# Attention: the diagonal blocks of the second pass masked by a bf16 product ahead of the exponential

## The reference, cut to what matters

```
att = einsum('bhqd,bhkd->bhqk', q, k) / scale
att = where(tril, att, -inf);  att = softmax(att, axis=-1)
y = einsum('bhqt,bhtd->bhqd', att, v)
x = x + (y @ Wo.T + bo)
```

## Time and profile before

| | us |
|---|---|
| median of 3 runs | 3162.8 |
| lowest and highest of them | 3155.71, 3166.08 |
| the profiled execution, its own time | 3170.36 |
| its span, first to last instruction | 3168.4 |
| the second pass of attention in it | 156 to 316.7 |
| TensorE busy | 2841.4 (90%) |
| VectorE, ScalarE, GpSimd busy | 1743.9, 1548.3, 361.7 |

### The profile page before, as it was taken

One profiled execution on the slowest core, in us unless ns is written; L12 is line 12 of the kernel. 1 busy time (PEld: TensorE's weight loads), 2 busy tenths in 40 slices (PEclk: granted clock), 3 DMA queues, 4 the chain that ended last, 5 costly groups with the idle time before them and its releaser, 6 DMA issues. The chain is left out here.

```text
span 3168.4 us, 79399 instructions
## 1 busy us (share of the span) xinstructions
PE 2841.4 (90%) x31700; PEld 2180.3 (69%) x31700; DVE 1743.9 (55%) x4255; ACT 1548.3 (49%) x3945; POOL 361.7 (11%) x731
## 2 busy tenths in 40 slices
PE   7899879999659999999999999989999998689998
PEld 4433559999526777677676677767767767579997
DVE  4443556666245556556555555655655555476663
ACT  1123222322136676677667667667666766422221
POOL 0011000000002111111111111111111111000000
PEclk9889889999779999999999999999999999889999
DMA  1000012010000000000000000000000000011100
GB/s 44 25 1 1 26 42 81 27 53 26 5 28 5 12 12 16 5 12 16 5 16 12 16 5 12 15 5 12 15 6 15 12 6 6 26 57 53 50 30 13
DMA packets 58891, 65.34 MB, mean 21 GB/s; under 512 B 16064, under 2 KB 50256, under 8 KB 58576
## 3 DMA queue, kind: packets, MB, share of 16 engines
q1 hardware_dynamic: 58576, 60.92, 6.2%
HBM read 59.86 MB, written 1.05 MB: 19 GB/s over the span
## 5 line engine op out<-in xcount | busy, mean ns | idle before, releaser
L1362 PE MATMUL dn_ps<-xnT,dn_w 128*128 128x512 f32 x768 | 378.9, 619 | 18.7 <-issue 11.5
L433 ACT ACTIVATE g_h<-g_ps,g_b_now 128x512 f32<-128x512 f32 x256 | 174.9, 688 | 338.3 <-PE g_ps L457 332.5
L1446 PE MATMUL dn_ps<-dn_zi,dn_wt 64*64 64x64 f32 x5120 | 262.3, 226 | 50.2 <-DVE dn_zi L1800 50.0
L470 PE MATMUL g_ps<-g_w_high,g_h_low 128*128 128x256 f32 x1024 | 290.3, 283 | 0.0
L470 PE MATMUL g_ps<-g_w_low,g_h_high 128*128 128x256 f32 x1024 | 290.2, 283 | 0.0
L470 PE MATMUL g_ps<-g_w_high,g_h_high 128*128 128x256 f32 x1024 | 290.1, 283 | 0.0
L1446 PEld LDWEIGHTS dn_ps<-dn_zi,dn_wt 64*64 64x64 f32 x5120 | 210.7, 139 | 77.1 <-DVE dn_zi L1800 51.9
L1800 DVE TENSOR_TENSOR dn_zi<-dn_ps,dn_mz 128x128 f32<-128x128 f32 x640 | 159.7, 286 | 186.3 <-PE dn_ps L1436 182.1
L1533 ACT ACTIVATE dn_qs<-dn_ps,dn_cf 64x128 f32<-64x128 f32 x448 | 162.3, 362 | 203.3 <-DVE dn_wv L1810 198.8
L1741 DVE SCALAR_TENSOR_TENSOR dn_cv<-dn_raw,dn_cw,dn_cv 128x1024 f32<-128x1024 f32 x192 | 247.5, 1289 | 2.0
L1810 DVE SCALAR_TENSOR_TENSOR dn_wv<-dn_ps,dn_cf,dn_vt 64x128 f32<-64x128 f32 x448 | 156.6, 349 | 147.8 <-PE dn_ps L1461 142.9
(11 more groups left out here) (267 smaller groups left out, 5980.2 us busy)
## 6 DMA issues: line engine op xcount, KB each, us to landing
g_w<-in_fc_dram SPq DMA_DIRECT2D x32, 1024.0 KB, 6.6
dn_w<-in_W_qkvz_dram SPq DMA_DIRECT2D x16, 768.0 KB, 4.4
dn_wout<-in_W_out_dram SPq DMA_DIRECT2D x16, 256.0 KB, 2.6
f_gate<-in_gateT_dram SPq DMA_DIRECT2D x16, 128.0 KB, 2.2
f_up<-in_upT_dram SPq DMA_DIRECT2D x16, 128.0 KB, 2.4
f_down<-in_downT_dram SPq DMA_DIRECT2D x16, 128.0 KB, 2.4
x_res<-in_x_dram SPq DMA_DIRECT2D x1, 1024.0 KB, 5.0
out_dram<-x_res SPq DMA_DIRECT2D x1, 1024.0 KB, 4.7
```

The costliest lines, as they stand in the source:

```text
L433: nc.scalar.activation(h[:, f % 4], h_b[f % 4], ACT.Gelu, bias=b1_now[u // 2][:, f:f + 1]).then_inc(h_ready, 1)
L470: last = pe.matmul(y_b[q % 2][:, 0:D], hidden[:, f, q * P:(q + 1) * P], weights[:, f, :], start=(f == 0 and n == 0), stop=(f == NF - 1 and ...
L1362: mm = pe.matmul(bA if where == "A" else bC, w[:, k, W_COL[u] * P:(W_COL[u] + 1) * P], m.xnT[:, k, b * T:(b + 1) * T], start=(k == 0), sto ...
L1446: mm = pe.matmul(block_of(bD[s], 1, b, h), wt[s][half(h), 1, b, :], zi[s][half(h), b, :], start=True, stop=True)
```

## The change

The table of constants gets an eighth block, the transposed causal mask. It is loaded and cast beside the first. The key side's scores leave their PSUM group open and two bf16 products, identity by transposed mask, are added onto the diagonal block ahead of the exponential; they give `sT_ready`. The masks of both sides become steps of their own, which stand behind both score products. GpSimd's loop of selections and its semaphore are gone; the value products wait for `e_ready`.

```diff
-    table = np.concatenate([eye, causal, tri, ones, last, last0, last1], axis=1)
+    table = np.concatenate([eye, causal, tri, ones, last, last0, last1, causal.T], axis=1)
...
+        maskT = sb("maskT", [P, P], BF16)
...
-            LOADS = 8 + 2 * HKV
+            LOADS = 9 + 2 * HKV
...
                 sp.dma_start(mask_in[:], const(table, C_CAUSAL)).then_inc(loaded, 16)
+                sp.dma_start(maskT_in[:], const(table, C_CAUSAL_T)).then_inc(loaded, 16)
...
                 nc.gpsimd.tensor_copy(mask[:], mask_in[:]).then_inc(padded, 1)
+                nc.gpsimd.tensor_copy(maskT[:], maskT_in[:]).then_inc(padded, 1)
...
+
+                def mask_rows(n):
+                    t = n % HT
                     for i in range(2):
                         mm = pe.matmul(slot(rows_place(n))[:, i, t * P:(t + 1) * P], ident[:], mask[:], start=False, stop=True)
                     mm.then_inc(s_ready, 1)
...
-                        mm = pe.matmul(slot(keys_place(n))[:, i, 0:T - j * P], kT[rows, b * T + j * P:b * T + (j + 1) * P],
-                                       qT[rows, r, b * T + j * P:(b + 1) * T], start=True, stop=True)
+                        pe.matmul(slot(keys_place(n))[:, i, 0:T - j * P], kT[rows, b * T + j * P:b * T + (j + 1) * P],
+                                  qT[rows, r, b * T + j * P:(b + 1) * T], start=True, stop=False)
+
+                def mask_keys(n):
+                    for i in range(2):
+                        mm = pe.matmul(slot(keys_place(n))[:, i, 0:P], ident[:], maskT[:], start=False, stop=True)
                     mm.then_inc(sT_ready, 1)
 
                 def values(n):
                     pair, b, r, gp, j = item(n)
-                    pe.wait_ge(p_ready, n + 1)
+                    pe.wait_ge(e_ready, n + 1)
...
                 for n in range(AHEAD):
                     rows_of_scores(n)
+                    mask_rows(n)
...
                         keys_of_scores(n)
                     if n + AHEAD < ITEMS:
                         rows_of_scores(n + AHEAD)
+                    if n < ITEMS:
+                        mask_keys(n)
+                    if n + AHEAD < ITEMS:
+                        mask_rows(n + AHEAD)
...
-                for n in range(ITEMS):
-                    pool.wait_ge(e_ready, n + 1)
-                    diagonal = pT[n % PT_BUFS][:, :, 0:P]
-                    nc.gpsimd.affine_select(diagonal, diagonal, [[0, 2], [1, P]], ALU.is_ge, 0.0, base=0,
-                                            channel_multiplier=-1).then_inc(p_ready, 1)
```

## The result

The changed kernel took 3179.78 us (median of 7 runs, 3173.06 to 3181.26) against 3166.08 (7 runs, 3155.71 to 3173.92): a ratio of 1.0042, 95% interval 1.0025 to 1.0059. A second set, with the changed kernel run again, gave 3176.17 against 3165.89, ratio 1.0032, interval 1.0017 to 1.0047. So the change costs 0.3 to 0.4% (the two intervals together reach from 0.2 to 0.6%), 13.7 and 10.3 us by the medians; 11.7 were forecast.

What follows compares the result with a forecast made beforehand. TensorE's list was taken to bound the pass. Mask products 9.1, stall 2.1 and load 0.45, less 0 for the selection, gave +11.7 us: 3162.8 to 3174.5 (+0.37%), range 3167 to 3184, 8 times in 10.

Steps and rivals of the forecast that it cites:

- The selection is free.: GpSimd's key-side selection, 26.0 us, runs beside other work; removing it gains 0, bounds 0 to 1.1 us.
- A pair of products costs 0.12, in items 54 to 63 0.22.: 128 mask products added on TensorE in the key pass: 9.1 us in sum, bounds 8.4 to 14.2.
- A late release costs 0.30 at seven steps, 2.1 us.: Exponentials released by the mask pair start later, so row scores wait for PSUM slots: 2.1 us, bounds 0 to 6.2.
- The load costs 0.45.: First block: the new mask's load, ahead of the biases, delays what follows by 0.45 us, bounds 0.2 to 0.9.
- Rival 1: Full-row masks bring the clock's rise to the key pass's start: -6.3 us, so +5.4, 3168; chance 0.1.
- Rival 2: Key pass: masks near their lower bound and no stall, +8.6 us, about 3171; chance 0.2.
- Rival 3: Key pass: weight loads set the pace and the slots stall more, +21.3 us, 3184; chance 0.15.
- Rival 4: GpSimd's selection held something the waits don't show, such as value products: +9.4 us at best; chance 0.05.

Runs made afterwards that it cites:

- key masks at once: The changed kernel with the key masks directly behind the key scores, ahead of the row scores: 3208.93 against 3163.94 us for the kernel before, ratio 1.0145.
- twelve ahead: The kernel before without row masks, with the row side 12 items ahead instead of 10: median 3150.41 against 3165.31 us for the kernel before, ratio 0.9951.

## Why the prediction was right

It was right in direction and size: +11.7 forecast, +13.7 and +10.3 measured, both medians (3179.8 and 3176.2) within the stated range, and the traces give +9.5 (second profile +9.2) in the pass and +0.5 ahead of it. So by the traces the sum was 1.8 us too high, and that the medians come out nearer to it is chance. The level was forecast as 3174.5 and measured as 3179.8; 3.3 of the 5.3 us between them lie in the kernel before, whose median went from 3162.8 with three runs to 3166.1 with seven. By the prediction's steps:

- *The selection is free.* Shown: without it the pass is 0.08 us shorter.
- *A pair of products costs 0.12, in items 54 to 63 0.22.* 0.11 in the steady steps, shown again by doubling them. In the last ten items 0.22 in seven of ten, but 0.00 at item 54, where the maxima set the end, -0.01 at 58, where the copy of the result did, and 0.07 at 59, where the turning follows, a product of the masks' own shape. This made 1.6 instead of 2.2. What was over-sized is the rule that every product in a full list adds its price; where another engine ends the step, it doesn't. The products by themselves cost 9.46 - 2.60 = 6.9 us, where 9.1 were forecast.
- *A late release costs 0.30 at seven steps, 2.1 us.* 0.30 at each of the six of full clock (2.25 - 1.84 - 0.11), hidden at items 14, 22 ... as said. With the release alone it is 0.35 there and 0.44 at item 2, at the slow clock, and the pass came to 2.6 more.
- *The load costs 0.45.* 0.48 by the traces, and the load alone repeats it.
- *Rival 1, an earlier clock.* Did not come. The clock rose at 187.4 us, 3.1 after the first value product (186.7 and 3.9 before). What I had not weighed is the other side: a rise 15.7 to 21.7 us after the first value product, which four other kernels of this study had in at least one profile (key masks at once, each of the two without row masks, twelve ahead). By an estimate from the late rise of the kernel before without row masks, which cost 6.0 us, the 3179.8 of the first set would have become 3186, outside the range, and the 3176.2 of the second 3182, inside it.
- *Rival 2, no stall.* The stall is there, in the size forecast. But of its other terms the masks came out below its 8.4, so the traced 9.9 lie between its 8.6 and the 11.7.
- *Rival 3, weight loads of 100 ns setting the pace.* Excluded by the doubled masks.
- *Rival 4, the selection held something unseen.* Excluded by leaving it out.
- *What I missed about the whole:* stages that the change doesn't touch, before and behind it, move by up to 5 us between executions, and the stages right behind it do so with the clock for the most part. Of the measured +13.7 the steps explain 9.9 (9.46 and 0.48), of +10.3 the second profile's 9.7. A single profile could not have told it: the first one's span grew by 11.1, the second one's by 5.5.

## What to carry to other kernels

An engine that has 26 us of work hidden beside the bound is not a cost, and moving the work onto the bound is one even at 0.055 us a product. In a ring of buffers, follow each signal that comes later to the slot that it frees: here a later signal alone cost 2.6 us, in one step of four, and could be worked out to the hundredth from four rows. Ask first whether the guarded work is needed at all: the masks that could go were those of the maximum.

## What the runs showed of the hardware

- A bf16 product of 128x128 followed by others of its shape costs 0.055 us at the full clock, the first after a change of tile shape 0.10 more; the weight loads of 98 to 100 ns run ahead and don't show.
- Two sets of f32 products in different row groups of 32 run fully beside each other: 256 columns and 128 columns take 0.63 us to the masks behind them (244.80 to 245.43), and 256 alone take 0.64 (306.12 to 306.76 in the changed kernel). Twelve items ahead instead of ten used that in every step, and gave 7.1 us.
- The granted clock of a stretch is not given by how busy TensorE is in the records. In this pass, which begins with score products of 32 rows, it stayed at 1.2 GHz for 24 to 51 us of nearly unbroken work, and in one and the same kernel it rose once at 179.9 and once at 194.7 us, which is 6.0 us of the pass. The first value products, of 128 rows, always came before the rise, by 2.5 to 21.7 us. What decides within that stays open.
